# Routing weight moved to the up projection's input and expert outputs summed in PSUM, with other planned lengths, in a four-layer decoder kernel

## The reference

```python
logits_BSE = jnp.einsum('BSD,DE->BSE', x, router_kernel_DE)
probs_BSE = jax.nn.softmax(logits_BSE.astype(jnp.float32), axis=-1)
weights_BSK, indices_BSK = jax.lax.top_k(probs_BSE, TOP_K)
norm_weights_BSK = jax.nn.softmax(weights_BSK, axis=-1)
one_hot_BSKE = jax.nn.one_hot(indices_BSK, num_classes=E, dtype=x.dtype)
full_weights_BSE = jnp.sum(one_hot_BSKE * norm_weights_BSK[..., None], axis=2)
gating_BSEF = jnp.einsum('BSD,EDF->BSEF', x, kernel_gating_EDF)
act_BSEF = jax.nn.silu(gating_BSEF)
up_BSEF = jnp.einsum('BSD,EDF->BSEF', x, kernel_up_EDF)
fuse_BSEF = act_BSEF * up_BSEF
down_BSED = jnp.einsum('BSEF,EFD->BSED', fuse_BSEF, kernel_down_EFD)
out_BSD = jnp.einsum('BSED,BSE->BSD', down_BSED, full_weights_BSE)
```

## Time and profile before

| | |
|---|---|
| median of 3 runs | 4889.51 us (4880.54 to 4900.06) |
| the profiled execution | 4887.98 us, its span 4885.9 us |
| TensorE busy | 3554.6 us, 73% |
| DVE busy | 2998.1 us, 61% |
| ACT busy | 2027.0 us, 41% |
| POOL busy | 1241.6 us, 25% |
| mean granted clock of TensorE | 0.83 of full speed |

### The profile page before, as it was taken

How to read it: one execution, slowest core, us unless ns; L and a number is a source line. 1 busy time by engine, 2 the same in 40 slices (tenths; PEclk the granted TensorE clock), 3 DMA queues, 4 the chain that set the end, 5 groups by cost and what they waited for, 6 DMA issues and landing times.

```text
span 4885.9 us, 78021 instructions
## 1 busy us (share of the span) xinstructions
PE 3554.6 (73%) x25546; PEld 2358.5 (48%) x25546; DVE 2998.1 (61%) x7047; ACT 2027.0 (41%) x3183; POOL 1241.6 (25%) x1568
## 2 busy tenths in 40 slices
PE   6768868566977787765885887876588688686655
PEld 4645545334655454432574555543366455453333
DVE  4535873885553686477555478377655558738834
ACT  2324445443343444544343354543433344454422
POOL 0001450550000343254000044145200014505500
PEclk7979988768988898786897988977789899887666
DMA  6020021313211012132212002122312200213121
GB/s 221 7 92 20 27 76 39 130 37 104 91 51 61 27 44 88 47 103 67 108 44 90 19 32 79 44 85 79 106 55 66 80 17 28 76 38 122 45 100 46
DMA packets 174979, 328.73 MB, mean 67 GB/s; under 512 B 13260, under 2 KB 114988, under 8 KB 173740
## 3 DMA queue, kind: packets, MB, share of 16 engines
q1 hardware_dynamic: 174572, 323.59, 19.5%
HBM read 231.87 MB, written 91.67 MB: 66 GB/s over the span
## 4 chain that ended last, share of the span: by engine, by line
PE 34%; issue 34%; DVE 15%; POOL 6%; ACT 5%; DMA 4%; SPq 1%; DVEq 0%; POOLq 0%; ACTq 0%
PE bank L1649 5%; PE bank L1660 3%; DVE sb_big L2097 3%; PE bank L1864 3%; POOL sb_rs L1417 2%; PE bank L971 2%; PE bank L492 2%; PE bank L547 2%; PE bank L919 2%; DVE sb_big L2102 2%; POOL sb_big L1993 2%; PE bank L992 1%; POOL sb_big L1980 1%; PE bank L974 1%; PE bank L566 1%
## 5 line engine op out<-in xcount | busy, mean ns | idle before, releaser
L1980 POOL TENSOR_TENSOR sb_big<-sb_big 128x512 f32<-128x512 f32 x384 | 494.7, 1303 | 278.9 <-DVE sb_big L2080 277.4
L1417 POOL TENSOR_TENSOR sb_rs<-sb_ve,sb_weights_const 128x4 f32<-128x4 f32 x112 | 113.9, 1017 | 1634.0 <-DVE sb_ve L1403 1634.0
L1864 PE MATMUL bank<-sb_big,sb_weights_const 128*128 128x512 f32 x512 | 377.1, 827 | 195.2 <-DVE sb_big L2102 194.7
L1941 ACT ACTIVATE bank<-sb_big,sb_Aneg 128x512 f32<-128x512 f32 x512 | 350.5, 687 | 385.4 <-DVE sb_big L2097 273.3
L2097 DVE TENSOR_TENSOR_SCAN sb_big<-bank,sb_big 128x512 f32<-128x512 f32 x384 | 465.1, 1211 | 5.1 <-POOL sb_big L1980 5.0
L1235 DVE TENSOR_REDUCE sb_small<-bank 128x4 f32<-128x308 f32 (+1 forms) x512 | 265.2, 524 | 328.9 <-PE bank L950 318.0
L971 PE MATMUL bank<-sb_big 128*77 128x128 bf16 (+1 forms) x2560 | 359.1, 232 | 129.5 <-DMA sb_big<-key_parts 57.5
L971 PEld LDWEIGHTS bank<-sb_big 128*77 128x77 bf16 (+1 forms) x2560 | 272.6, 116 | 217.8 <-issue 155.9
L1120 ACT ACTIVATE sb_big<-bank 77x512 f32<-77x512 f32 (+1 forms) x352 | 208.0, 592 | 268.2 <-PE bank L992 178.8
L950 PE MATMUL bank<-sb_big 128*128 128x77 bf16 (+1 forms) x2048 | 187.3, 226 | 159.1 <-DMA sb_big<-query_parts 100.6
L974 PE MATMUL bank<-sb_topT,sb_pick 128*77 128x128 bf16 (+1 forms) x2048 | 301.4, 228 | 0.0
(11 more groups left out here) (339 smaller groups left out, 8180.5 us busy)
## 6 DMA issues: line engine op xcount, KB each, us to landing
sb_big<-query_parts SPq DMA_DIRECT2D x160, 512.0 KB, 6.6
sb_big<-state_rows SPq DMA_DIRECT2D x128, 512.0 KB, 3.7
query_parts<-sb_big SPq DMA_DIRECT2D x120, 384.0 KB, 3.3
sb_big<-key_parts SPq DMA_DIRECT2D x64, 512.0 KB, 8.9
sb_big<-context_key_parts SPq DMA_DIRECT2D x64, 308.0 KB, 3.8
key_parts<-sb_big SPq DMA_DIRECT2D x48, 384.0 KB, 4.4
context_key_parts<-sb_big SPq DMA_DIRECT2D x48, 231.0 KB, 4.0
sb_big<-masked_key_parts SPq DMA_DIRECT2D x32, 308.0 KB, 3.5
```

Source lines behind the costliest of these rows:

```text
L1864: pe.matmul(m.bank[s][2][:, :], m.const["ident"], M.h(s, 2 * (n % 2)), start=n == 0, stop=n == NS - 1)\
L1941: act.activation(M.dA(s, half), M.dl(s, half), ACT.Exp, scale=m.Aneg[:, NS * half + n:NS * half + n + 1])\
L1980: pool.tensor_tensor(M.h(s, 2 * (n % 2) + half), M.b_rows(s, n // 2)[:, n % 2, :], M.du(s, half), ALU.mult)\
```

## The change

In L0f alone:

- cw is transposed on TensorE (4 transposes, as in L1f), copied to SBUF by ACT, written to DRAM (16 KB) and read back by 4 transfers that spread two experts' rows each over all 128 partitions. Both kinds of transfer are in SP's queue.
- GpSimd multiplies each expert's row with xT (8 instructions of 128x512 f32), and the up matmuls read this product in place of xT. They wait for it.
- One matmul of zeros opens bank 3, and the down matmuls of all 8 experts accumulate there. The DVE adds bank 3 to x once at the end (1 instruction of 128x512) in place of 32 of L1729.
- The first expert stands at 0.3 of the sublayer in place of 0.2.

In the whole kernel the planned lengths are others. The semaphores of the quantised network take the names of those of the experts, which changes no instruction and no wait.

```diff
     def time(self, e, f):
 
-        return 0.2 + 0.8 * (e * self.ft + f) / ((E + 1) * self.ft)
+        first = 0.3 if self.gated else 0.2
+        return first + (1.0 - first) * (e * self.ft + f) / ((E + 1) * self.ft)
...
-                    pe.matmul(m.bank[s][k][:, :], X.w(name, lo, lo + 128), m.xT[s][:, :], start=True, stop=True)\
+                    if name == "up":
+                        pe.wait_ge(*g.at("ff_p", (X.key, e)))
+                    src = X.rows(s, e, e + 1)[:, 0, :] if name == "up" else m.xT[s][:, :]
+                    pe.matmul(m.bank[s][k][:, :], X.w(name, lo, lo + 128), src, start=True, stop=True)\
                       .then_inc(*g.one("ff_pe", (X.key, name, e, f)))
...
+                    if e == 1 and X.gated:
+                        pe.matmul(m.bank[s][3][:, :], m.zerob[:, :], m.identb[:, None, :].to_broadcast([128, NB, T]),
+                                  start=True, stop=False)
...
-                                     start=(f == 0), stop=(f == X.ft - 1))
+                                     start=f == 0 and not X.gated,
+                                     stop=f == X.ft - 1 and (not X.gated or (e == E and b == NB - 1)))
...
+def experts_sp(sp, g, m, X):
+    s = g.s
+    yield 0.185
+    sp.wait_ge(*g.at("ff_a", (X.key, "cwT")))
+    sp.dma_start(m.dw[s], X.cwT(s)).then_inc(*g.landing("wb", X.key))
+    yield 0.21
+    sp.wait_ge(*g.landed("wb", X.key))
+    for pair in range(E // 2):
+        if pair >= 2:
+            sp.wait_ge(*g.landed("rb%d" % (pair % 2), (X.key, pair - 2)))
+        sp.dma_start(X.rows(s, 2 * pair, 2 * pair + 2), m.dw[s][None, 2 * pair:2 * pair + 2, :].to_broadcast([128, 2, N]))\
+          .then_inc(*g.landing("rb%d" % (pair % 2), (X.key, pair)))
+
+def experts_pool(pool, g, m, X):
+    s = g.s
+    for e in range(E):
+        yield X.time(e, -0.8)
+        if e == 0:
+            pool.wait_ge(*g.at("ln_xT", X.key))
+        if e % 2 == 0:
+            pool.wait_ge(*g.landed("rb%d" % (e // 2 % 2), (X.key, e // 2)))
+        row = X.rows(s, e, e + 1)[:, 0, :]
+        pool.tensor_tensor(row, row, m.xT[s][:, :], ALU.mult).then_inc(*g.one("ff_p", (X.key, e)))
...
-        if e >= 1:
+        if X.gated:
+            if e == E:
+                yield X.time(E, X.ft - 0.1)
+                dve.wait_ge(*g.at("dn_pe", (X.key, E - 1)))
+                dve.tensor_tensor(m.x[s].rearrange("p b d -> p (b d)"), m.bank[s][3][:, :],
+                                  m.x[s].rearrange("p b d -> p (b d)"), ALU.add)\
+                   .then_inc(*g.one("dn_d", (X.key, E - 1)))
...
-SPAN = {"L0a": 94, "L0x": 32, "L0f": 90, "L1a": 151, "L1x": 107, "L1f": 135, "L2a": 345,
-        "L2x": 112, "L2f": 34, "L3a": 126, "L3x": 104, "L3f": 92}
+SPAN = {"L0a": 89, "L0x": 20, "L0f": 63, "L1a": 151, "L1x": 107, "L1f": 135, "L2a": 341,
+        "L2x": 112, "L2f": 30, "L3a": 113, "L3x": 124, "L3f": 47}
```

More of the change, by code:

```diff
@@ L214 @@
     rt_pe="PE: router", rt_d="DVE: router", rt_a="ACT: router",
-    ff_pe="PE: hidden tile", ff_a="ACT: hidden tile", ff_d="DVE: hidden tile", dn_pe="PE: expert's output",
+    ff_pe="PE: hidden tile or its parts", ff_a="ACT: hidden tile or its parts",
+    ff_d="DVE: hidden tile or its parts", ff_p="Pool: input times the routing weight", dn_pe="PE: expert's output",
     dn_d="DVE: expert's output added",
@@ L219 @@
     sc_in="Pool: a state's input", sc_y1="Pool: state added to the second half's y",
-    qf_pe="PE: quantised network", qf_a="ACT: quantised network", qf_d="DVE: quantised network",
-    qf_p="Pool: quantised network",
 )
 LANDINGS = dict(
-    wb="rows of B are in DRAM", rb0="an even pair of rows of B is on all partitions",
-    rb1="an odd pair of rows of B is on all partitions",
+    wb="rows of B or of routing weights are in DRAM", rb0="an even pair of these rows is on all partitions",
+    rb1="an odd pair of these rows is on all partitions",
     wq="query parts are in DRAM", wk="key parts are in DRAM", wm="the masked keys' row is in DRAM",
@@ L1619, in experts_pe @@
     s = g.s
-    if not X.gated:
-        yield 0.18
-        pe.wait_ge(*g.at("rt_d", (X.key, "cw")))
-        g.wait_free(pe, free, s, 0)
-        for b in range(NB):
-            last = pe.transpose(m.bank[s][0][0:E, b * T:(b + 1) * T], cut(m.small[s], 160, NB, E)[:, b, :],
-                                m.const["ident"])
-        last.then_inc(*g.one("ff_pe", (X.key, "cwT")))
-        free[s, 0] = ("ff_a", (X.key, "cwT"))
+    yield 0.18
+    pe.wait_ge(*g.at("rt_d", (X.key, "cw")))
+    g.wait_free(pe, free, s, 0)
+    for b in range(NB):
+        last = pe.transpose(m.bank[s][0][0:E, b * T:(b + 1) * T], cut(m.small[s], 160, NB, E)[:, b, :],
+                            m.const["ident"])
+    last.then_inc(*g.one("ff_pe", (X.key, "cwT")))
+    free[s, 0] = ("ff_a", (X.key, "cwT"))
+    if not X.gated:
         yield 0.19
@@ L2243, in quantised_pe @@
                                     Q.qb(s, b - 1)[:, 128 * j:128 * j + 128], m.identb[:, :])
-            last.then_inc(*g.one("qf_pe", ("back", b - 1)))
-            free[s, 2] = ("qf_a", ("qT", b - 1))
+            last.then_inc(*g.one("ff_pe", ("back", b - 1)))
+            free[s, 2] = ("ff_a", ("qT", b - 1))
     yield 0.98
     g.wait_free(pe, free, s, 3)
-    pe.wait_ge(*g.at("qf_a", ("qT", NB - 1)))
+    pe.wait_ge(*g.at("ff_a", ("qT", NB - 1)))
     for b in range(NB):
@@ L2252, in quantised_pe @@
                              m.w2t[:, 128 * j:128 * j + 128], start=j == 0, stop=j == 3)
-    last.then_inc(*g.one("qf_pe", "out"))
+    last.then_inc(*g.one("ff_pe", "out"))
     free[s, 3] = ("x_upd", "L3f")
@@ L2282, in quantised_pool @@
             last = pool.memset(Q.hp(s, j)[:, :, at:at + 1], 0.0)
-    last.then_inc(*g.one("qf_p", "pad"))
+    last.then_inc(*g.one("proj_p", ("L3f", "pad")))
 def quantise_tokens_dve(dve, g, m, Q):
@@ L2290, in step @@
     def step(name, last):
-        last.then_inc(*g.one("qf_d", name))
+        last.then_inc(*g.one("ff_d", name))
     def after(name):
-        dve.wait_ge(*g.at("qf_d", name))
+        dve.wait_ge(*g.at("ff_d", name))
     yield 0.02
@@ L2634, in sublayer @@
                     yield from heads_pool(pool, g, m, S[key])
+                if key == "L0f":
+                    yield from experts_pool(pool, g, m, X[key])
                 if key == "L2a":
@@ L2690, in sublayer @@
                     yield from heads_sp(sp, g, m, S[key])
+                if key == "L0f":
+                    yield from experts_sp(sp, g, m, X[key])
                 if key == "L2a":
```

70 lines of the change are left out of this document (37 added, 33 removed).

## The result

The changed kernel takes 4988.09 us (median of 4, 4981.98 to 5001.12), the one before 4891.1 us beside it (4880.54 to 4900.06): ratio 1.02, 95% interval 1.0177 to 1.0223. It is 97 us slower; 45 us faster was forecast.

What follows compares the result with a forecast made beforehand. No engine was full; stretches with different limits, and waits, bounded the kernel. 4 x (-6 - 7) + 3 x (10 - 10) + 7 = -45 us from 4888.0 gave 4843 us; range 4750 to 4925.

Steps and rivals of the forecast that it cites:

- The lengths in the second part: Second part, three times: new planned lengths make L1x's stretch denser, -10 us each, bounds 0 and -20.
- the 65% that I named as the sign: Second part: the stretch of L1x and L3f was to have TensorE busy over 65%.
- The way to be wrong that I had named: L3f, squeezed to 47 units, ends long after L1x, so stream 0's L1f waits for it in TensorE's queue.
- The DVE's relief: First part, four times: 10.3 us less DVE work for each L0f gives -7 us, bounds 0 and -20.
- The exchange of waits in the first part: L0f's stretch, four times: TensorE's idle 21.9 us become 15.6, 6.8 of it new wait; -6 us, bounds 0 and -13.
- the 20 us that I named as a sign: First part: L0f's stretch shorter by some 20 us, much of it coming back beside L1a.
- The chain: L0f's routing weight to first up matmul: 8.3 us behind cw; new waits 6.8 us per first part, 12 per second.
- the sum of +10: Second part, three times: 10.4 us new waits, about 2 given back, 1.7 for TensorE's slower clock; +10 us.
- Alone: Stream 0 alone at the start, once: first up matmul at 99.9 us, +7 us.
- The chain costs more than it frees: Rival, 18%: each L0f waits 21.8 us uncovered, 8 x 21.8 - 120 = +54, 4942 us.
- The lengths bring more: Rival, 20%: TensorE's idle time falls to 14%, 20 us more per first part, 10 per second; -127, 4761 us.
- The DVE gains nothing: Rival, 20%: the DVE waits out GpSimd's 64 products, 83 us, so the -7 falls away; 4871 us.

Runs made afterwards that it cites:

- e2: Kernel before with the new planned lengths and nothing else changed: 4945.63 us, ratio 1.0099.
- e19: e11 with L3x planned at 79 and L3f at 92 in the second part only: 4884.01 us, 0.998 of the kernel before.
- e11: Changed kernel keeping in L0f only the PSUM sum and first expert at 0.3 (no routing weight, chain or products), new lengths: 4919.9 us, ratio 1.0048.
- e13: Kernel before with the first expert at 0.3 in place of 0.2 and nothing else: 4946.47 us, ratio 1.0103.
- e15: e11 with the first expert back at 0.2, new lengths kept: 4922.59 us, ratio 1.0058.
- e14: e1 with the first expert back at 0.2: 4970.82 us, 1.0159 of the kernel before.
- e1: Changed kernel with the old planned lengths: 4943.74 us, 1.01 of the kernel before.
- e12: e6 with the first expert back at 0.2, old lengths kept: 4874.35 us, 0.9959 of the kernel before.
- e6: Changed kernel keeping in L0f only the PSUM sum and first expert at 0.3 (no routing weight, chain or products), old lengths: 4923.79 us, ratio 1.0062.
- e17: e4 without GpSimd's 64 products; transposes, copy and transfers stay: 4955.59 us, 1.013 of the kernel before.
- e5: e4 with the old planned lengths: 4923.16 us, 1.0075 of the kernel before.
- e4: Changed kernel whose up matmuls read xT and wait for no product; products still made, routing weight left out of the result: 4959.54 us, ratio 1.0123.

## Why the prediction was wrong

**The lengths in the second part** are the step that failed most: half of the 20 us that a denser stretch would give, -10 each; measured +22.6 (e2). I saw that 45% of L3x moves beside L1x and argued from the idle share there. That stretch fell short of the 65% that I named as the sign (63%), and took 116 us, not under 74. The idle time was not room: the stretch lasts until stream 1's chain of L3x and L3f is through, about 170 us behind L3x's start before and after, since L1x's output stands behind L3f's last matmul. What the new lengths changed is when L3x starts: 25 us later in e2, 32 in the changed kernel. The way to be wrong that I had named, L3f squeezed and ending long after L1x, has the right queue, but L3f takes the same 44 to 45 us as before. With 79 and 92 (e19) L3x gets shorter than in the kernel before, and each second part 8 us shorter than e11's. The medians differ by 36 us, of which the traces have 16 in the first parts, whose table is the same. That L3x is late because L3a is late is where the times point. No experiment that moved L3a, L3x and nothing of stream 0 was made, so this cause stays argued.

**The first expert at 0.3** I had not costed at all: +54 us by itself (e13), 0 with the new lengths (e15, e11), -27 with the chain under the old ones (e14, e1). Under the new lengths it was harmless to the sum alone; with the chain and the new lengths it was not tried. Nor can e1's 50 us be put down to it: without the 0.3 e1 is slower still (e14), since the chain then has less cover.

**The DVE's relief** was forecast at 28 us in the first parts, from 82 us less work. The 82 were too many: they took each of 32 additions at 0.343 us, but four in a row take 1.13 us and not 1.37, as they overlap. By e12's trace 72 us of additions went and 5.5 us of new ones came, and the DVE is busy 2935.3 us, 63 less than before. The sum alone gives 18 us in all, with the waits for x (e12). In the changed kernel the DVE's busy time does not fall, since L1408 takes 60 us more.

**The exchange of waits in the first part** was right for its place and wrong for its worth. The stretch of the changed kernel that answers to the earlier trace rows:

```profile
PE bank L1431 <- DVE sb_xn L1408: 4.9, 1, 4.9
PE bank L492 <- ACT sb_xT L1441: 4.5, 1, 4.5
PE bank L1656 <- POOL sb_big L1703: 3.5, 1, 3.5
PE bank L1629 <- DVE sb_small L1584: 2.0, 1, 2.0
PE bank L1431 <- DVE sb_xT L1408: 1.6, 1, 1.6
```

The wait for L2a's norm fell from 9.1 to 1.6 us, as said, and the new ones are 3.5 + 2.0, a little under my 6.8. The 4.9 + 4.5 us lie behind L0f's end (1710), where L1a begins; the earlier trace rows ends at L0f's end and leaves the like stretch out, in which 6.0 us of waits stood. But the exchange is not the work of the new chain: e2, with the new lengths and without the chain, has no wait for L2a's norm in this stretch either, and the same 4.9 + 4.5. Its L0f lasts 70 us in a first part, the changed kernel's 72, and before it was 90, so the 20 us that I named as a sign came, with the lengths. They are given back behind L1f of stream 1, since stream 0 is the later for it (L2a begins 137 us into a first part in e2, 121 before). Of -13 us for each first part 2.3 came, and e2 has 3.6: the change to L0f itself gave nothing there.

**The chain.** All of the change to L0f costs 7 us in a second part with the old lengths (e1 382.3, before 375.4) and 8.4 with the new (406.4, e2 398.0), so the sum of +10 had the right size, by luck of its terms: with the new lengths the chain by itself is 13.8 (e11 392.6), where I had 12, and the sum in PSUM gives back 5; with the old ones the chain is 1.6 (e6 380.7) and the rest is the 0.3. The new waits, forecast at 75 us, are 50. **Alone** the forecast was 7 and 18 came. The first up matmul starts 4.9 us later than forecast, of which 4.2 are the write to DRAM (5.8 for 1.6), and L0f is 11.8 us longer than before: 7 + 4.9. The other 6.6 us lie in L1a, which takes 97.5 us for 90.9; it takes 97.7 in e2 too, so this comes with the lengths and not with the chain.

**The rivals.** "The chain costs more than it frees" gave the time that lies nearest, 4942 us, and its name came true, though not by its working. I had an L0f wait 21.8 us uncovered, 174 us in all, against 120 freed. With the new lengths the chain costs 68 us (e11 to the changed kernel) and the sum in PSUM frees 26 (e2 to e11), so the change to L0f is 42 us slower by itself; with the old lengths and the first expert at 0.2 it is 96 (e12 to e14) against 18. So for the new lengths the new waits were priced about right (75 for 68), and what the change frees far too high (90, without the 30 of the lengths, for 26). "The lengths bring more" had the wrong sign. "The DVE gains nothing" had the right mechanism: GpSimd's operation does hold up the DVE. For the 64 products it is shown to be worth 4 us (e17), within the error, not 28. The range, 4750 to 4925, left out the case that the lengths and the change to L0f are each slower by some 50 us. (The 4800 to 4864 given for the forecast alone do not follow either: its terms' bounds, all to one side, add up to 4733 and 4925.)

**Adding up**, in one order of several. From 4892: the sum -18 (e12), the 0.3 +50 (e6), the products with their chain 0 (e5), the wait +20 (e1) give 4944. By the new lengths: e11 4920, transposes, transfers and products +40 (e4), the wait +29 give 4988. The +40 is 12 alone, 2 in each first and 7 in each second part; 4 of it are the products. Why transposes and transfers cost 7 us in each second part under the new lengths and nothing under the old ones is open; L3a starts 4 us later in e4's pass than in e11's (134.4 and 130.1). No version with the whole computation was faster than the kernel before.

## What to carry to other kernels

An idle share in a stretch where two chains meet need not be room. Here the stretch lasted until one chain was through, 170 us behind the start of its last attention, and what counted was when that started. The sign to look for is which chain ends last there and what stands behind it in the queue. In a table of planned times every number is an edit of its own, a position as much as a length, and its worth depends on the others (0.3: +50, 0 and -27 us here); try each alone, and each part of the program apart. A sum of busy time taken from an engine is worth what it frees on the path, here 18 us for 63. And two halves that add up to the whole are no proof that they are independent: e1's half is made of parts that the whole does not have.

## What the hardware showed

The forecast said that the DVE's durations are never lengthened by GpSimd, from two rows of operations with two inputs from SBUF. The DVE's f32 operation of 128x128 with one tensor input, SBUF to SBUF, is: in place of 0.34 us it takes 1.18 to 1.46 beside a GpSimd operation of 128x512, 69 times in the changed kernel and 8 times in the kernel before. That GpSimd is the cause is shown for xT: its longest is 1454 ns with the 64 products and 346 without them (e17). The Trainium skill (SBUF — State Buffer, SBUF: two separate sides) says that the pair of ports which the two share is locked for the whole instruction, also for DVE operations in a mode that uses two ports, and not only for those with two SBUF inputs; the trace agrees if L1408 is one of these, which no row tells. The forecast took only the second half of that rule. The 25 that the products hold cost nothing that can be told (e17 against e4); what the 36 that Mamba's operations hold more than before cost, no run separates from the lengths.
